# Row sums and squares for two layer norms, and a three-pass output product, in an RWKV kernel on one core

## What is computed

```
ffn(x)  = sum_k w[k] * (x @ W[ids[k]].T + b[ids[k]])
x1 = x + 0.5 * ffn(layernorm(x))
u  = layernorm(x1)                       # the block's input
h  = layernorm(u) * ln1_g + ln1_b ;  hh = h one token earlier
k, v, r = (h*tm + hh*(1-tm)) @ Wk.T, Wv.T, Wr.T
rwkv = sigmoid(r) * wkv(time_decay, time_first, k, v)     # a scan over tokens
a  = u + rwkv @ Wo.T
g  = layernorm(a) * ln2_g + ln2_b ;  gg = g one token earlier
kk = relu((g*cm_k + gg*(1-cm_k)) @ Wck.T) ** 2            # 1024 wide
x2 = x1 + a + sigmoid((g*cm_r + gg*(1-cm_r)) @ Wcr.T) * (kk @ Wcv.T)
out = x2 + 0.5 * ffn(layernorm(x2))
```

## Time and profile before

| | |
|---|---|
| median of 3 runs | 436.53 us (435.98 to 436.53) |
| profiled execution, its own time | 435.98 us |
| its span | 434.2 us |
| busy: PE, DVE, ACT, POOL | 419.3, 380.5, 305.9, 179.1 us |
| share of the span | 97%, 88%, 70%, 41% |
| round 3 (206.60 to 253.90): busy PE, DVE, ACT, POOL | 46.91, 45.29, 37.39, 22.28 us |
| round 6 (348.50 to 395.70): the same | 47.20, 41.48, 33.55, 15.51 us |
| statistics of x1 on DVE in round 3 | 241.95 to 244.00 |

### The profile page before, as it was taken

How to read it: one execution, slowest core, us unless ns; L and a number is a source line. 1 busy time by engine, 2 the same in 40 slices (tenths; PEclk the granted TensorE clock), 3 DMA queues, 4 the chain that set the end, 5 groups by cost and what they waited for, 6 DMA issues and landing times. The chain is left out here.

```text
span 434.2 us, 6241 instructions
## 1 busy us (share of the span) xinstructions
PE 419.3 (97%) x2042; PEld 336.1 (77%) x2042; DVE 380.5 (88%) x779; ACT 305.9 (70%) x573; POOL 179.1 (41%) x164
## 2 busy tenths in 40 slices
PE   8989988989999999999999999999999999999996
PEld 8855865668868887798769886888779876988985
DVE  3989989999999999999999999999999999976235
ACT  1158977896689677994789668967797478945420
POOL 1545053626281646344462728154643346033011
PEclk9999999999999999999999999999999999999998
DMA  6991010001000200011000200010001000000101
GB/s 209 385 396 54 2 48 0 2 2 51 0 0 2 97 2 1 0 51 48 2 0 26 74 0 2 0 51 0 2 0 49 2 0 2 30 19 1 49 2 49
DMA packets 15971, 18.52 MB, mean 43 GB/s; under 512 B 1082, under 2 KB 13634, under 8 KB 15938
## 3 DMA queue, kind: packets, MB, share of 16 engines
q1 hardware_dynamic: 14538, 17.05, 11.1%
q10 hardware_dynamic: 1400, 1.07, 0.8%
HBM read 13.92 MB, written 4.19 MB: 42 GB/s over the span
## 5 line engine op out<-in xcount | busy, mean ns | idle before, releaser
L477 PE MATMUL pair<-wcv_sb,kk 128*128 128x256 f32 x448 | 100.4, 380 | 0.0
L477 PEld LDWEIGHTS pair<-wcv_sb,kk 128*128 128x128 f32 x448 | 83.8, 190 | 11.3 <-ACT kk L717 0.6
L1282 POOL TENSOR_TENSOR x2b<-xs,bias_bc 128x512 f32<-128x512 f32 (+1 forms) x16 | 20.1, 1256 | 92.4 <-DVE xs L1100 48.6
L451 PE MATMUL pair<-xck_hi,wck_hi 128*128 128x512 f32 x128 | 54.3, 424 | 0.0
L455 PE MATMUL pair<-xck_lo,wck_hi 128*128 128x512 f32 x128 | 50.6, 395 | 0.0
L452 PE MATMUL pair<-xck_hi,wck_lo 128*128 128x512 f32 x128 | 50.6, 395 | 0.0
L713 ACT ACTIVATE kk<-pair 128x512 f32<-128x512 f32 x64 | 36.4, 591 | 20.0 <-PE pair L455 19.8
L1282 POOL TENSOR_TENSOR x<-x,bias_bc 128x512 f32<-128x512 f32 x14 | 18.1, 1295 | 63.4 <-DVE rwkv L1016 36.3
L1322 POOL TENSOR_TENSOR xs<-x,xa 128x512 f32<-128x512 f32 x16 | 20.4, 1274 | 44.9 <-DVE xa L1022 44.3
L717 ACT ACTIVATE kk<-kk 128x512 f32<-128x512 f32 x64 | 35.9, 626 | 0.0
L1262 POOL TENSOR_TENSOR rstd_x<-vare_x,nhalf 128x4 f32<-128x4 f32 (+2 forms) x26 | 30.1, 1157 | 8.9 <-DVE vare_x L876 7.4
(11 more groups left out here) (159 smaller groups left out, 1069.3 us busy)
## 6 DMA issues: line engine op xcount, KB each, us to landing
x<-in_x_dram SPq DMA_DIRECT2D x8, 512.0 KB, 3.5
out_dram<-xs SPq DMA_DIRECT2D x15, 256.0 KB, 2.1
...
```

The costliest lines, as they stand in the source:

```text
L451: nc.tensor.matmul(key_bank(n), wck_hi[:, h, cols], xck_hi[:, h, :], start=h == 0, stop=False)
L477: last = nc.tensor.matmul(bank_of("kv", e, i)[:, t % TB * C:(t % TB + 1) * C], kk[:, n, tok:tok + P], wcv_sb[:, n, :], start=n == 0, stop= ...
L1282: nc.gpsimd.tensor_tensor(dst, tile, bias_bc[:, :].rearrange("p (a c) -> p a c", a=1).broadcast_to([P, tiles, C]), ALU.add).then_inc(done, 1)
```

## The change

Three things are changed.

1. *The output product* of sequences 1 to 7 becomes three fp32r passes. ScalarE copies each half of `rwkv` to `rwkv_hi` (in the place of `xr`), VectorE subtracts (`rwkv_lo`, in the place of `rwkv`). On TensorE it moves behind six parts of the first value tile instead of four. On ScalarE `channel_gate` is split: bank 0, squares 4 and 5, `rwkv_hi`, bank 1, `residual_of`, squares 6 and 7. wo is split once, at the start, `wo_hi` taking the place of constants that only the setup uses.
2. *Statistics of x1* of sequences 2 to 7: `add_first` also writes row sums; GpSimd scales them (`lower`), ScalarE makes squares with row sums, GpSimd makes the variance and roots. `stats_x1` goes from VectorE for these.
3. *Statistics of x2* of sequences 0 to 5: the last addition of `value_sum` is four instructions with row sums instead of two without; ScalarE squares two tiles among the relus and two behind square 0. The root moves on GpSimd from the start of the round to behind `hold_exponents`.

Beside these, GpSimd's second bias addition to x1 waits for `rwkv_lo_done`, and the second half of `add_second` stands behind `add_output`. The core of the diff:

```diff
+    SUMS_X1 = 2
+    SUMS_X2 = B - 2
...
+wo_hi, wo_lo = in_place_of("early", "wo_hi", [P, CH, C]), in_place_of("wo_sb", "wo_lo", [P, CH, C])
...
+rwkv_hi, rwkv_lo = in_place_of("xr", "rwkv_hi", [P, CH, T]), in_place_of("rwkv", "rwkv_lo", [P, CH, T])
...
     def output_product(f):
         if f == 0:
             pe.wait_ge(s_wo, 1)
-        pe.wait_ge(rwkv_done, 2 * f + 2)
-        to_tokens("o", rwkv, wo_sb, xa2_done, f, o_ps)
+            pe.wait_ge(rwkv_done, 2 * f + 2)
+            to_tokens("o", rwkv, wo_sb, xa2_done, f, o_ps)
+            return
+        if f == 1:
+            pe.wait_ge(s_wo_lo, 1)
+        pe.wait_ge(rwkv_lo_done, 2 * (f - 1) + 2)
+        for i in range(BANKS):
+            take(pair_of("o", f), i, xa2_done, 2 * f + i + 1)
+            for t in range(TB):
+                last = three_passes(bank_of("o", f, i)[:, t * C:(t + 1) * C], i * TB + t, rwkv_hi, rwkv_lo, wo_hi, wo_lo)
+            last.then_inc(o_ps, 1)
...
-        channel_values(e, 0, range(HB // 2))
+        channel_values(e, 0, range(HB - 2))
         if has(f):
             output_product(f)
-        channel_values(e, 0, range(HB // 2, HB))
+        channel_values(e, 0, range(HB - 2, HB))
         channel_values(e, 1)
...
+    def output_input_high(f):
+        act.wait_ge(r_ps, 2 * f + 2)
+        for h in range(CH):
+            act.wait_ge(rwkv_done, 2 * f + h + 1)
+            nc.scalar.activation(rwkv_hi[:, h, :], rwkv[:, h, :], ACT.Copy).then_inc(rwkv_hi_done, 1)
...
+    def row_squares(kind, tile, i, t, f):
+        act.wait_ge(lowered_done[kind], i + 1)
+        if t == 0:
+            act.wait_ge(gated_done, 2 * f + 2)
+        nc.scalar.activation(eb_v[:, t // TB, t % TB * C:(t % TB + 1) * C], tile[:, t, :], ACT.Square, scale=ROOT, bias=lowered[kind][:, t:t + 1],
+                             accum_out=var_of[kind][:, t:t + 1]).then_inc(var_done[kind], 1)
...
+    def squares_x1(b):
+        for t in range(NT):
+            row_squares("x1", x1[b % X1], b - SUMS_X1, t, b - 1)
+    def squares_x2(e, tiles):
+        for t in tiles:
+            row_squares("x2", xs[e % XS], e, t, e + 1)
...
+        if 0 <= e - 1 < SUMS_X2:
+            squares_x2(e - 1, (0,))
         key_relu(e, 2)
+        if 0 <= e - 1 < SUMS_X2:
+            squares_x2(e - 1, (1,))
         key_relu(e, 3)
...
-        channel_gate(e)
+        channel_gate(e, (0,))
+        for n in range(HB // 2, HB - 2):
+            key_square(e, n)
+        if has(f):
+            output_input_high(f)
+        channel_gate(e, (1,))
         if has(f):
             residual_of(f)
-        for n in range(HB // 2, HB):
+        for n in range(HB - 2, HB):
             key_square(e, n)
+        if has(f + 1):
+            squares_x1(f + 1)
...
-                last = nc.vector.scalar_tensor_tensor(tile[:, t, :], product[:, t % TB, :], rstd_x[b % 2][:, t:t + 1],
-                                                      tile[:, t, :], ALU.mult, ALU.add)
+                last = nc.vector.scalar_tensor_tensor(tile[:, t, :], product[:, t % TB, :], rstd_x[b % 2][:, t:t + 1], tile[:, t, :], ALU.mult, ALU.add,
+                                                      accum_out=sums["x1"][:, t:t + 1] if b >= SUMS_X1 else None)
...
+            if b >= SUMS_X1:
+                last = nc.vector.tensor_scalar(normed[:, t, :], x1[b % X1][:, t, :], negm[:, t:t + 1], rboth[:, t:t + 1], ALU.add, ALU.mult)
+                if t % TB == TB - 1:
+                    last.then_inc(normed1, 1)
...
+    def output_input_rest(f, h):
+        dve.wait_ge(rwkv_hi_done, 2 * (f - 1) + h + 1)
+        nc.vector.tensor_tensor(rwkv_lo[:, h, :], rwkv[:, h, :], rwkv_hi[:, h, :].bitcast(F32), ALU.subtract).then_inc(rwkv_lo_done, 1)
...
+        if e < SUMS_X2:
+            for t in range(i * TB, (i + 1) * TB):
+                last = nc.vector.scalar_tensor_tensor(xs[e % XS][:, t, :], xs[e % XS][:, t, :], 1.0, thc[:, t, :], ALU.mult, ALU.add,
+                                                      accum_out=sums["x2"][:, t:t + 1])
+            last.then_inc(x2_done, 1)
+            return
         nc.vector.tensor_tensor(tok_bank(xs[e % XS], i), tok_bank(xs[e % XS], i), tok_bank(thc, i), ALU.add).then_inc(x2_done, 1)
...
+        if has(f):
+            output_input_rest(f, 0)
         if has(e - 1):
             add_second(e - 1, 0)
-            add_second(e - 1, 1)
+        if has(f):
+            output_input_rest(f, 1)
         if has(f + 1):
             add_first(f + 1)
         if has(f):
             add_output(f)
-        if has(f + 1):
+        if has(f + 1) and f + 1 < SUMS_X1:
             stats_x1(f + 1)
+        if has(e - 1):
+            add_second(e - 1, 1)
         if has(f):
             norm_output(f)
         if e == LAST:
...
+    def lower(kind, i, done, count):
+        pool.wait_ge(done, count)
+        nc.gpsimd.tensor_scalar(lowered[kind][:, :], sums[kind][:, :], -ROOT / C, None, ALU.mult).then_inc(lowered_done[kind], 1)
+    def add_eps(kind, i):
+        pool.wait_ge(var_done[kind], NT * (i + 1))
+        nc.gpsimd.tensor_scalar(vare[kind][:, :], var_of[kind][:, :], EPS, None, ALU.add).then_inc(vare_done[kind], 1)
...
+        if b >= SUMS_X1:
+            add_eps("x1", b - SUMS_X1)
+            nc.gpsimd.tensor_scalar(both[:, :], var_of["x1"][:, :], EPS * EPS / (1.0 + EPS), None, ALU.add).then_inc(both_done, 1)
+            pool.wait_ge(both_done, b - SUMS_X1 + 1)
+            nc.gpsimd.tensor_scalar(negm[:, :], sums["x1"][:, :], -1.0 / C, None, ALU.mult).then_inc(negm_done, 1)
+            inverse_root(rboth[:, :], both[:, :], nhalf[:, :], rboth_done)
+            pool.wait_ge(vare_done["x1"], b + 1)
+            inverse_root(rstd["x1"][:, :], vare["x1"][:, :], nhalf[:, :], rstd_done["x1"])
+            pool.wait_ge(rstd_done["x1"], b + 1)
+            nc.gpsimd.tensor_tensor(shift1[:, :], negm[:, :], rstd["x1"][:, :], ALU.mult).then_inc(shift1_done, 1)
...
+        if 0 <= e - 1 < SUMS_X2:
+            lower("x2", e - 1, x2_done, 2 * (e - 1) + 2)
         if has(e - 1):
             bias_to_x2(e - 1, 1)
+        if e - 1 >= SUMS_X2:
             inverse_std("x2", e - 1)
...
+        if 0 <= e - 1 < SUMS_X2:
+            add_eps("x2", e - 1)
+            inverse_std("x2", e - 1)
         if has(f + 1):
             pool.wait_ge(aa_done, 2 * f + 2)
             bias_to_x(f + 1, 0)
-            pool.wait_ge(rwkv_done, 2 * f + 2)
+            pool.wait_ge(rwkv_lo_done, 2 * (f - 1) + 2)
             bias_to_x(f + 1, 1)
+        if has(f + 1):
+            lower("x1", f + 1 - SUMS_X1, x1_done, 2 * (f + 1) + 2)
```

More of the change, by code:

```diff
@@ L106, in build @@
         shift1 = sb("shift1", [P, NT])
+        sums = {k: sb(f"sums_{k}", [P, NT]) for k in ("x1", "x2")}
+        lowered = {k: sb(f"lowered_{k}", [P, NT]) for k in sums}
+        var_of = {k: sb(f"var_of_{k}", [P, NT]) for k in sums}
         mean_x = sb("mean_x", [P, NT])
@@ L374, in ffn_setup @@
                 pe.wait_ge(s_bias_sel, 16 * K)
-                nc.tensor.matmul(pair[0][:, 0, 0:C], gate_rows[:, :], bias_sel[:, :], start=True, stop=True).then_inc(s_bias_ps, 1)
+                nc.tensor.matmul(pair[0][:, 0, 0:C], gate_rows[:, :], bias_sel, start=True, stop=True).then_inc(s_bias_ps, 1)
                 pe.wait_ge(s_ffn_acc, K)
@@ L378, in ffn_setup @@
                     for h in range(CH):
-                        last = nc.tensor.matmul(pair[0][:, 1, a * C:(a + 1) * C], (centre_own if a == h else centre_other)[:, :], ffn_sum[:, h, :],
+                        last = nc.tensor.matmul(pair[0][:, 1, a * C:(a + 1) * C], (centre_own if a == h else centre_other), ffn_sum[:, h, :],
                                                 start=h == 0, stop=h == CH - 1)
@@ L865, in aggregate @@
             def aggregate(kind, b, tiles=range(NT), part=0):
-                dve.wait_ge(bn_done[kind], b + part + 1)
+                made = (b - SUMS_X2 if kind == "x2" else b) + part + 1
+                dve.wait_ge(bn_done[kind], made)
                 if b > 0 and part == 0:
@@ L871, in aggregate @@
                 last.then_inc(mv_done[kind], 1)
[L872 removed]
+                dve.wait_ge(mv_done[kind], made)
                 some = slice(tiles[0], tiles[-1] + 1)
```

38 lines of the change are left out of this document (27 added, 11 removed).

## The result

The changed kernel takes 443.87 us (median of 4 runs, 443.57 to 444.93), the kernel before 436.47 (435.98 to 436.53): 1.018 times as long, 95% interval 1.016 to 1.019. The forecast was 445.8 in a range of 438.0 to 451.0. The profiled execution took 443.67 us, with a span of 441.7.

A forecast was written before the change was run, and what follows sets the result against it. TensorE, busy 97% of the span, was taken to bound the kernel, with VectorE's longer chain behind rwkv deciding after the change: 1.24 + 7.35 + 1.18 = 9.8 us on 435.98 gives 445.8 us, range 438.0 to 451.0.

The forecast's parts named there:

- Wait before the product: TensorE before the output product: waits 1.40 us for rwkv_lo and starts 2.26 us later than before.
- GpSimd's addition against `add_first`: VectorE's add_first meets GpSimd's bias addition in every round, one instruction stretched, 2.60 us for the four.
- Accumulator reads: VectorE's reads of row sums in add_first: 0.10 us each, three exposed, 0.3 us; bounds 0 and 0.3 each.
- From `xa` to `norm_output` to the values: Chain behind add_first: 3.53 us to GpSimd's root, 1.07 to norm_output, 2.14 more to the value records.
- What goes at no price: Removed VectorE statistics (x1 2.05 us a round, x2 1.9), added squares and wo's split were taken to leave the time unchanged.
- wrong if `rwkv` comes earlier against the front products: Sign against the forecast: rwkv's end was held tied to TensorE's front products through ScalarE and GpSimd.
- Rounds 0 and 6: First and next-to-last rounds: round 0 longer by 1.24 us, round 6 by 1.18.
- The start: Copy of wo and its rest at the start, beside waits: 0 to 0.5 us, taken as 0.
- the root beside the denominators: Rival, 5%: GpSimd's root for x2 keeps out VectorE's denominators, rwkv 0.7 us later in rounds 1 to 6; 450.0 us.
- the accumulating form: Rival, 5%: accumulating VectorE instructions run at half the pace, 1.2 us in each of rounds 0 to 5; 453.0 us.
- one idle piece: TensorE's only gap in old round 3, 0.24 us before the transposes of normed.
- The first rival, that TensorE keeps its saving: Rival, 12%: rwkv's rest is ready by 236.70, all rounds give 0.61 us; 431.7 us.

The follow-up runs named there:

- e4: Changed kernel without the bias addition to the last two token tiles of x1 of sequences 2 to 7; 439.47 us.
- e8: Changed kernel with GpSimd's bias addition to the second bank of x1 moved to the start of the round; 440.32 us.
- e1: Changed kernel with only the three-pass product and its order, statistics of x1 and x2 made on VectorE as before; 458.89 us.
- e11: e2 with the statistics of x2 put back to VectorE's statistics instruction, those of x1 new; 432.2 us.
- e9: Changed kernel with both rwkv rests ahead of add_second, rwkv copies behind square 4, and the bias placed as in e8; 435.83 us.
- e5: Changed kernel with GpSimd's bias additions to both banks of x1 made some 9 us sooner, the first beside VectorE's scans; 447.2 us.
- e2: Changed kernel with only the new statistics, output product in fp32 as before, second half of add_second kept behind add_output; 431.45 us.
- e10: e2 with the bias placed as in e8; 431.8 us.

## Why the prediction was right

Direction, mechanism and place were right, and 7.4 us came where 9.8 were forecast. In the profiles rounds 0 to 6 are 6.8 us longer; another 0.8 lie at the start, where the forecast had nothing, and bring the sum nearer to it by luck. By its steps:

- *Wait before the product.* Forecast 3.98 us from the start of the values to the product, measured 3.82. It is released by `rwkv_lo`, as said. Right, 0.16 too long; the idle row shows 1.07 us of it, where 1.40 was forecast.
- *The product.* Forecast 2.84 us, measured 241.60 to 244.55 = 2.95.
- *GpSimd's addition against `add_first`.* One L987 of 1.51 us (forecast: the 1486 ns of round 0), in every round; e4 and e8 confirm the cause.
- *Accumulator reads.* This term was mis-sized. Taken at 0.10 us each on the pace, 0.3 exposed; they cost about 0.01: L987 goes at 0.41 us from start to start, against 0.40 for L923. `add_first` took 2.66 us, not 2.90, and in e1, where it meets GpSimd too but writes no sums, 2.63. That is 0.24 us in each of six rounds, 1.4 us in all.
- *From `xa` to `norm_output` to the values.* 4.59 and 2.15 us, forecast 4.60 and 2.14.
- *What goes at no price.* This step failed by the prediction's own sign, "wrong if `rwkv` comes earlier against the front products": `rwkv` came 0.26 us earlier against them. The chain through GpSimd, on which nothing was to change, got shorter: `mix_r` took 2.54 us in place of the 2.81 of the earlier trace rows. It lies beside `xv_lo` on VectorE, a subtraction of two SBUF tiles, for 0.27 us in place of 0.53. The statistics of x2 make this: `mix_r` takes 2.82 us in e1 and e11 too, where they are made as before, and 2.54 in all kernels with the new ones. Together with the reads this makes a round +0.95 us in place of +1.47.
- *A second meeting.* The prediction missed one. GpSimd's addition for x2 (212.03, 1.59 us) now lies beside the two L1030 on VectorE, which take 2.45 us in place of 1.41. It costs the round nothing, because behind it VectorE waits 0.74 us for ScalarE's exponentials, as it did before (0.73).
- *Rounds 0 and 6.* 1.08 and 1.04 us, forecast 1.24 and 1.18.
- *The start.* 0.8 us longer, taken as 0. VectorE ended the sum of the adapter weights at 14.1 us in place of 13.3, behind later DMAs. In the profile of e9, which has all of the change's work at the start, that point lies at 13.5 and the product of sequence 0 starts at 50.65, against 50.44 before; in the other profiles it lies as late as 14.6. So most of it looks like a difference between executions; that isn't shown by repeats.

Of the rivals, the root beside the denominators costs nothing (two L1051 take 1.29 us with GpSimd's root of x2 beside them), and the accumulating form does not run at half the pace. The view by source line of after (minimum, median and maximum in ns):

```profile
L987 DVE SCALAR_TENSOR_TENSOR x<-y1s,rstd_x,x x16: 474/476/1512, 96.8 to 243.7; 128x256 f32<-128x256 f32 x16
L987 DVE DVE_READ_ACCUMULATOR x<-y1s,rstd_x,x x16: 76/77/83, 97.2 to 244.1; 128x1 f32 x16
```

476 ns with the sums, 474 without. The Trainium skill ("Vector Engine (DVE) Microarchitecture Reference", Points that are easy to get wrong) has this form at half throughput; the trace disagrees, for 256 elements in fp32. The lock that the Trainium skill has between VectorE with two SBUF inputs and GpSimd ("SBUF — State Buffer", Who interferes with whom) agrees with the 1512 ns of L987 and with e5's scans, not with roots of four elements.

One reading was wrong though it did not move the forecast: the "one idle piece" of 0.24 us. TensorE's loss to `norm_output` was 0.8 us a round, a part of it inside the transposes. Whoever reads 0.24 must think that new statistics can give at most 0.24 us a round to the old kernel, under 2 us in all; e2 shows 5.4. The first rival, that TensorE keeps its saving, underrated for the same reason what the statistics are worth, and overrated the product: 2.4 us of copies and rests (1.15 + 1.28) for 0.5 us of TensorE's work.

**A better version.** e2, the new statistics with the old product, takes 431.45 us: 1.2% less than before and 2.8% less than after. With e10 (431.8) it is the fastest of all that ran. What the product in three passes would bring with nothing in its way was not reached by any run.
